# Tokenizer tower on one core: the weight stage's residual conv as column-half pairs, image stores in pieces

## The reference, cut to what matters

```python
x = patches(x)                      # 784 patches of 3x16x16, normalised by their own mean and deviation
x = conv3x3(x, conv1_w) ; residual = x
x = gelu(group_norm(x)) ; x = conv3x3(x, rconv1_w)
x = gelu(group_norm(x)) ; x = conv3x3(x, rconv2_w)
x = residual + x
x = conv(x, proj_w, stride=16)      # 192 numbers a patch
... embeddings, one causal attention block, one two-branch transformer block
```

## Time and profile before

| what | us |
|---|---|
| median of 3 runs | 1586.49 (1581.76 to 1587.44) |
| profiled execution | 1585.12 |
| its span, first to last instruction | 1583.3 |
| first matmul of the weight stage | 14.24 |
| last matmul of the weight stage ends | 246.2 |
| first conv1 of the main stage | 248.96 |
| PE busy over the span | 1429.4 (90%) |

### The profile page before, as it was taken

One profiled execution on the slowest core, in us unless ns is written; L12 is line 12 of the kernel. 1 busy time (PEld: TensorE's weight loads), 2 busy tenths in 40 slices (PEclk: granted clock), 3 DMA queues, 4 the chain that ended last, 5 costly groups with the idle time before them and its releaser, 6 DMA issues. The chain is left out here.

```text
span 1583.3 us, 42709 instructions
## 1 busy us (share of the span) xinstructions
PE 1429.4 (90%) x13490; PEld 1008.6 (64%) x13490; DVE 1134.6 (72%) x4227; ACT 837.4 (53%) x2102; POOL 581.8 (37%) x1111
## 2 busy tenths in 40 slices
PE   6969996888999999989999998999999766978889
PEld 2424442333688588858877875888588666655647
DVE  7723334999988888888888887888888750474710
ACT  1212222777777676766767666666767501333442
POOL 2000003555544455444454544445554401161500
PEclk9989997999999999999999999999999887987999
DMA  6463325433555455445545553554555577300000
GB/s 181 122 205 88 99 87 220 100 101 101 138 148 143 123 150 143 131 121 145 144 119 151 146 140 101 149 147 128 139 144 143 160 202 167 71 1 1 2 3 14
DMA packets 117219, 190.63 MB, mean 120 GB/s; under 512 B 18252, under 2 KB 86284, under 8 KB 116942
## 3 DMA queue, kind: packets, MB, share of 16 engines
q1 hardware_dynamic: 117070, 188.60, 43.6%
HBM read 103.34 MB, written 21.30 MB: 79 GB/s over the span
## 5 line engine op out<-in xcount | busy, mean ns | idle before, releaser
L363 POOL TENSOR_TENSOR sb_tmp<-sb_mst,sb_half_neg 128x8 f32<-128x8 f32 x200 | 354.6, 1773 | 684.4 <-DVE sb_mst L789 684.4
L501 PE MATMUL rc<-sb_acts,sb_rwd 128*64 128x512 f16 x1764 | 563.5, 392 | 18.3 <-DMA sb_acts<-sb_hst 18.2
L502 PE MATMUL rc<-sb_acts,sb_rwd 128*64 128x512 f16 x1764 | 564.7, 393 | 0.0
L417 ACT ACTIVATE sb_f32q<-c,sb_gsh,sb_gsc 128x128 f32<-128x128 f32 x792 | 298.2, 458 | 285.6 <-POOL sb_gsh L373 285.6
L501 PE MATMUL rc<-sb_acts,sb_rwl 128*64 128x512 f16 x1176 | 363.9, 391 | 5.2 <-issue 5.2
L502 PE MATMUL rc<-sb_acts,sb_rwl 128*64 128x512 f16 x1176 | 363.4, 391 | 0.0
L556 PE MATMUL pj<-sb_wall,sb_arena 128*64 128x384 f16 x1792 | 309.9, 337 | 21.7 <-DMA sb_wall<-w_lo 15.1
L425 ACT ACTIVATE sb_g2f<-rc,sb_gsh,sb_gsc 128x128 f32<-128x128 f32 x784 | 297.3, 481 | 4.4 <-POOL sb_gsh L373 4.4
L560 PEld LDWEIGHTS pj<-sb_wall,sb_arena 128*64 128x64 f16 x1792 | 219.0, 222 | 63.8
L560 PE MATMUL pj<-sb_wall,sb_arena 128*64 128x192 f16 x1792 | 240.9, 247 | 0.0
L556 PEld LDWEIGHTS pj<-sb_wall,sb_arena 128*64 128x64 f16 x1792 | 215.5, 219 | 38.8 <-DMA sb_wall<-w_lo 16.4
(11 more groups left out here) (158 smaller groups left out, 1726.2 us busy)
## 6 DMA issues: line engine op xcount, KB each, us to landing
sb_acts<-sb_hst SPq DMA_DIRECT2D x792, 78.8 KB, 2.6
sb_wall<-w_lo SPq DMA_DIRECT2D x56, 528.0 KB, 3.8
sb_im<-x_planes SPq DMA_DIRECT2D x202, 136.5 KB
sb_wall<-w_lo SPq DMA_DIRECT2D x28, 480.0 KB, 3.7
sb_f32q<-in_proj SPq DMA_DIRECT2D x12, 576.0 KB, 3.9
sb_arena<-in_proj SPq DMA_DIRECT2D x12, 576.0 KB, 4.4
w_lo<-sb_arena SPq DMA_DIRECT2D x1, 6144.0 KB, 17.3
scratch_fold<-sb_wall SPq DMA_DIRECT2D x48, 123.8 KB
```

The source lines that it names most:

```text
L363: ch.did(gp.tensor_tensor(t1, var, half_neg[:, :], ALU.pow))
L417: ins = nc.scalar.activation(g1f[:, q * Q + m, :], c1[q][:, m * HALF:(m + 1) * HALF], ACT.Gelu, bias=gsh[q][:, m:m + 1], scale=gsc[q][:, m ...
L501: nc.tensor.matmul(out[0:CH, :], w_odd, x_odd, start=(n == 0), stop=(n == 14))
L502: yield nc.tensor.matmul(out[CH:128, :], w_even, x_even, start=(n == 0), stop=(n == 14))
```

## The change

- **Residual conv** (`fold_pairs`): for each half, 15 pairs of matmuls in place of 18. Each pair is one matmul into partitions 0 to 63 of the bank and one into 64 to 127, each with 64 columns of weights. The first 6 pairs read only the low rows (slot 2 of `acts[p]`). The other 9 read the high rows, which stand in `acts[p]` doubled: slot 0 holds the image rows of one parity in both partition halves, slot 1 those of the other.
- **High rows**: ACT makes them now (`proj_hi`), into one buffer `hfull` for all units. SP copies them by four transfers of 64 partitions x 1296 (`double_proj`). DVE keeps the low part alone. `proj_hi` waits for the unit's load, and that the unit before has been split and doubled; in ACT's loop it stands between the two evacuations of `rc` and those of the projection. PE waits for the doubling (`s_fdup`) after the sixth pair of half 0.
- **SP** is written out for all units: double n + 1, load n + 2, store n.
- **Image stores** in 21 pieces: three for `scratch_x` after the stores of units 5, 6, 7, and eighteen of one plane each, one or two after each of units 9 to 20. The zero tiles come after unit 22. DVE splits the planes in three portions.
- **Weights**: two more transfers of parameters; `fdup` and `tdup` are doubled forms. POOL clears `hfull` and slot 2 at the stage's end.

```diff
-            def fold_io(i, p, last):
-                n = 2 * i + p
-                if not last:
-                    sp.wait_ge(s_psp, 2 * n + 2)
-                    load_proj(n + 2, p)
+            def double_proj(n):
+                p = n % 2
+                sp.wait_ge(s_psh, n + 1)
+                if n >= 2:
+                    sp.wait_ge(s_tps, n - 1)
+                for row, half in ((0, 0), (1, 1), (0, 1), (1, 0)):
+                    sp.dma_start(acts[p][64 * half:64 * half + 64, row, 0:U * PAD],
+                                 hfull[64 * row:64 * row + 64, :]).then_inc(s_fdup, 16)
+
+            def store_t(n):
+                p = n % 2
                 sp.wait_ge(s_tev, 3 * n + 3)
...
+            double_proj(0)
+            for n in range(FU - 1):
+                double_proj(n + 1)
+                if n + 2 < FU:
+                    sp.wait_ge(s_psp, n + 1)
+                    load_proj(n + 2, n % 2)
+                store_t(n)
+                if 5 <= n < 8:
+                    store_piece(n - 5)
+                if 9 <= n < 21:
+                    for m in range(18 * (n - 9) // 12, 18 * (n - 8) // 12):
+                        store_piece(C + m)
...
+            def proj_hi(i, p, wait=True):
+                n = 2 * i + p
+                act.wait_ge(s_pld[p], 16 * (i + 1))
+                if wait:
+                    act.wait_ge(s_psp, n)
+                    act.wait_ge(s_fdup, 64 * n)
+                nc.scalar.activation(hfull[:, :].rearrange("p (r x) -> p r x", x=WD * Q)[:, :, Q:(P + 1) * Q],
+                                     stage[p].rearrange("p (r x) -> p r x", x=P * Q), ACT.Copy, scale=WS).then_inc(s_psh, 1)
...
+                if more:
+                    proj_hi(i + 1, p)
                 if not first:
                     act.wait_ge(s_ts[p], 32 * i)
                 act.wait_ge(s_tps, n + 1)
...
+                    conv = fold_pairs(rc[p][q], acts[p], q)
+                    run(conv, 6)
+                    if q == 0:
+                        pe.wait_ge(s_fdup, 64 * (n + 1))
+                    run(conv).then_inc(s_fold, 1)
...
-                v.tensor_scalar(hi, src, WS, None, ALU.mult).then_inc(s_psp, 1)
-                dve.wait_ge(s_psp, 2 * n + 1)
                 v.scalar_tensor_tensor(lo, src, WS, hi, ALU.mult, ALU.subtract).then_inc(s_psp, 1)
```

More of the change, by code:

```diff
@@ L95, in build_front @@
         acts = [sb(f"acts_{i}", [128, 3, HB], F16) for i in range(2)]
[L96 to L97 removed]
+        hfull = sb("hst", [128, U * PAD], F16)
+        hst = [hfull[:, q * Q * PAD:(q + 1) * Q * PAD] for q in range(2)]
         g2f = sb("g2f", [128, U, HALF])
@@ L258, in load_im @@
                                          ap=[[1, 3], [PLANE, 18], [1, RUN]])).then_inc(s_im[p], 16)
[L260 to L263, removed]
+            sp.wait_ge(s_scr, 16 * STORES)
             load_im(0, 0)
             load_im(1, 1)
-            for p in range(2):
-                fold_io(FU // 2 - 1, p, True)
+            store_t(FU - 1)
             sp.wait_ge(s_wlo, 2 * FU)
@@ L468, in _ @@
         def _(pe):
[L469 to L480, removed]
             def run(gen, count=None):
@@ L502, in pairs, with fold_pairs, rows, wl @@
                     yield nc.tensor.matmul(out[CH:128, :], w_even, x_even, start=(n == 0), stop=(n == 14))
+            def fold_pairs(out, buf, q):
+                def rows(k, t, m):
+                    v = buf[:, k, q * Q * PAD:(q + 1) * Q * PAD].rearrange("p (r x) -> p r x", r=SL)
+                    return v[:, t:t + 8, m * Q:(m + P) * Q]
+                def wl(kind, m):
+                    return fwl[:, (3 * kind + m) * CH:(3 * kind + m + 1) * CH]
+                def wd(ky, m):
+                    return fwd[:, (3 * ky + m) * CH:(3 * ky + m + 1) * CH]
+                low = ((wl(0, m), rows(2, 1, m), wl(2, m), rows(2, 0, m)) for m in range(3))
+                edge = ((wl(1, m), rows(2, 0, m), wl(3, m), rows(2, 1, m)) for m in range(3))
+                odd, even = ((1, 0), (0, 1), (1, 1)), ((0, 0), (1, 0), (0, 1))
+                high = ((wd(ky, m), rows(*odd[ky], m), wd(ky, m), rows(*even[ky], m)) for ky in range(3) for m in range(3))
+                for n, (w_odd, x_odd, w_even, x_even) in enumerate(itertools.chain(low, edge, high)):
+                    nc.tensor.matmul(out[0:CH, :], w_odd, x_odd, start=(n == 0), stop=(n == 14))
+                    yield nc.tensor.matmul(out[CH:128, :], w_even, x_even, start=(n == 0), stop=(n == 14))
             def fold_step(i, p, first):
                 n = 2 * i + p
-                pe.wait_ge(s_psp, 2 * n + 2)
+                pe.wait_ge(s_psp, n + 1)
                 for q in range(2):
@@ L726, in _, with image_split @@
             dve.wait_ge(s_xz, 1)
-            for q in range(6):
+            def image_split(q):
                 c, pr = q // 2, q % 2
@@ L735, in _ @@
                 v.tensor_tensor(dst[1], src, dst[0], ALU.subtract).then_inc(s_xhl, 1)
-            with dve.Fori(2, FU // 2 - 1) as i:
+            for i in range(2, 5):
+                image_split(2 * i - 4)
+                image_split(2 * i - 3)
+                fold_pair(i)
+            with dve.Fori(5, FU // 2 - 1) as i:
                 fold_pair(i)
@@ L1524, in layout @@
     o["tband"] = tb.reshape(128, TP)
+    o["tdup"] = np.stack([np.concatenate([tb[h], tb[h]]) for h in range(2)], 1).reshape(128, 2 * TP)
     wb = np.zeros((KC, 2, CH), w1.dtype)
```

117 lines of the change are left out of this document (66 added, 51 removed).

## The result

| what | before | after |
|---|---|---|
| median of 4 runs each, us | 1584.85 (1581.76 to 1587.44) | 1626.13 (1622.69 to 1630.80) |
| ratio, 95% interval | | 1.0263 (1.0225 to 1.0302) |
| profiled execution | 1585.12 | 1629.21 |
| its span | 1583.3 | 1627.4 |
| weight stage ends | 246.2 | 281.4 |

The change costs 2.6%. I forecast 1620; it is 1626, inside the range, and 9.2 us above the forecast if profiled executions are compared. The span is 44.1 us longer: 35.2 of it stand in the weight stage, 3.2 in the gap before conv1, 5.7 behind it.

The account below looks back on a forecast made before the run. A chain from load to load through ACT and SP, 10.1 us, bounds the weight stage; 21 of these, the start, the last unit and 18 us of pieces end it 34.9 us later: 1585.12 becomes 1620 us, range 1597 to 1650.

Parts of the forecast that it names:

- The bound moves into a ring: Weight stage: a chain from one load's issue through ACT and SP to the next load's, 10.1 us (9.4 to 11.0).
- The backlog: Weight stage: each load stands behind four doublings in the queue, 0.4 us (bounds 0 and 1.3).
- The pieces: Weight stage: 21 image-store pieces on SP between a store and the doublings, 18 us (10 to 25).
- The start: Start of the weight stage: first preparing operation at 9.0 instead of 7.71, load of unit 2 issued at 32.2.
- The end: Weight stage's end to the main stage's first conv: nothing longer; about 8 us on SP fits beside unit 23.
- the cold start: Weight stage: after the tensor engine's idle at the seventh pair, a lower clock costs 2.0 us, taken by slack; nothing.
- slack as told: Weight stage: the tensor engine's work on a unit ends 5.9 us before ACT's next work could wait for it.
- Rival 3: Weight stage: the clock falls at the new wait and stays down, unit 11.4 us, 1647 us; chance 0.12.
- Rivals 1 and 2: Weight stage: tensor engine stays the bound, 1561 us, chance 0.05; or cheap doubling issue and no backlog, 1579 us, chance 0.08.

Follow-up runs that it names:

- the engine-bound version: Kernel after with the projection evacuated first, two of four doublings made as DVE copies, and zero tiles after units 8 and 21: 1550.44 us, ratio 0.9778.

## Why the prediction was right

**The bound moves into a ring: right.** Loads come 9.87 us apart, against 10.1. The terms, from the unit shown: landing with its wake-up and backlog 4.33 (forecast 4.1 + 0.4 + 0.1), high rows and evacuations 1.82 (1.94; the high rows alone 1.16, forecast 1.17), to SP 0.03 (0.21), stores 0.82 (0.79), doublings and step 2.44 (2.61). The landing varies most, and this ring has the shortest of the five: their mean until ACT may begin is 4.70, forecast 4.6. That each link is one is shown by the runs that take it out (evacuation, two doublings), not by the sum. One reading of the old kernel was off without harm: the load issued at 221.84 is that of unit 23, which the engine needs one unit after 228.43, so 15 us later and not 7.

**The backlog: a term that hit by luck.** I put 0.4 us on the load for standing behind four doublings, and the mean landing is about that much longer than in the earlier trace rows. But without two of them it landed no sooner, and in front of them 2 us later. What makes it longer is open.

**The pieces: mis-sized.** 18 us forecast, 24.3 measured (22.0 with the plain ring of 9.98), near the upper bound of 25. The three of `scratch_x` lengthened their rings by 8.1 (37.7 for three rings against 3 x 9.87), the ring after them by 0.7, the eighteen planes theirs by 15.5, or 0.86 each, where the price by bytes was 0.91. I had put my value between issue and bytes; bytes was the answer, and most of it is paid on SP: behind a `scratch_x` piece the doublings take 1.8 us longer to issue. With two planes in a ring, SP needs 1.3 us more from store to load (146.86 to 150.62, against 2.44), and the ring is about 1.9 longer.

**The start: 1.5 us too late.** 8.38 instead of 9.0, small transfers from 12.99, the first load in the ring at 30.68, not 32.2. The order of events was as told.

These errors cancel, which is luck: the start -1.5 us, the plain rings -4.8, the pieces +6.3. Twenty-one rings and the pieces took 231.6, forecast 230.1, and the load of unit 23 went out at 262.27, forecast 262.3; the stage ended at 281.4, forecast 281.1.

**The end: this step failed.** Up to the first conv "nothing gets longer by my reckoning", I wrote; it was 3.2 us longer. The chain from the store of unit 22 to conv1 is 0.76 for the store, 2.80 for the zero tiles, 1.28 until they have landed, 3.12 for issuing the image loads and 4.42 until conv1 starts, together 12.4. I had 0.79, 3.0, 2.6 and 2.6, which is 9.0, and nothing for the landing of the image windows. The chain also began later. By my own numbers unit 22 is through 8.7 us after the load of unit 23, at 271.0, and its store goes out behind the doublings, near 272.5, which would just have fitted. It went out at 274.99, 6.4 us before the stage's end: unit 22, at a granted clock of 0.50 in its first 5 us, took 8.6 us from its first high pair where I had 6.3. Twelve pairs at 0.42 instead of 0.22 are 2.4 us of that, an estimate from the rows of the profile that no run separates. So the cold start, which I put at nothing, costs nothing within the rings, but here, behind the last load, nothing covers it. In the three kernels with four of the zero tiles after unit 8 conv1's idle time is 2.8 again, released by DVE; in the kernels of the new order without that it is 4.6 to 6.3.

**Behind conv1: 5.7 us that I didn't forecast, most of it not told from spread.** From conv1 to the end the profiles of the new order take between 1332.6 and 1342.8 us (the kernel after 1340.0), the two of the old order 1334.3. What all of the new order share is a slower beginning: the first pair that needs high rows comes 20.16 us after conv1 instead of 18.43 (19.4 to 21.2 in the others). The 6 MB of low weights are in the queue there, landing in 22.6 us instead of 17.3, and the granted clock over the first 24 us is 0.50 instead of 0.64. Which of the two it is, no run shows.

**The tensor engine: slack as told.** It is idle 26 of 120 us. The granted clock fell in many units (0.89 over the stretch) and up to the last units nothing came later for it: ACT's evacuation of the projection waits for the engine only twice, 0.2 us each, in units 22 and 23. Rival 3 needed a unit of over 10.1 and did not come. Rivals 1 and 2 fell with the ring itself: issuing a doubling costs 0.60, not 0.38. Rival 1's sum, 1561, lies near what the engine-bound version reached (1550), which shows the distance that was at stake.

## What to carry to other kernels

When an edit adds a step between a transfer's landing and the next transfer's issue, follow the order lists around in a circle and add up the links; if the circle is longer than the busiest engine's unit, it sets the time, however idle each engine is. Then look for what stands in the circle only by its place in a list: moving one evacuation ahead of a wait was worth 59 us here, and took the stores and pieces with it. What follows the last round of the circle needs a sum of its own, down to the last landing: there the slack that covers a late engine inside the circle is gone. Half of a doubling that stays in its own partitions is a copy, not a transfer.

## What the runs showed of the hardware

**First in the queue is not first to land.** A load of 576 KB with four doublings of 162 KB ahead of it on the same queue landed in 4.3 to 4.4 us (evacuation first), and in 6.5 to 7.7 with the doublings right behind it; the doublings themselves went from 2.9 to 4.5. Counted from the first of the five issues to the last landing the two orders are near each other: 2.4 + 4.9 = 7.3 in the kernel after, and 7.5 to 8 in the one with the load first. It looks as if all five ended together when the load goes first. The Trainium skill, "DMA: Bandwidth & Descriptors", section "Queues, rings and completion order", says that descriptors are consumed in ring order but that completion is not first in, first out for an issuing engine. The second half agrees with these landings: the first doubling is issued 0.6 us behind the load and lands after 4.5, the load after 6.5 to 7.7. The first half alone would not let me expect that a later transfer delays an earlier one by 2 to 3 us. Why it does is open.

**Issuing is held up by what is in flight.** Four doublings take 2.39 us to issue, 4.19 behind a piece of 784 KB, eight of them 15.61 while the image load runs and 8.36 otherwise (with a wait for the second unit's high rows in both). Rival 1 of the prediction cites the Trainium skill, "DMA: Bandwidth & Descriptors", section "Issuing engines are not separate DMA queues", that issuing is usually small beside the transfer. For one doubling that is so here (0.60 us, against 3.4 to landing). But four stand one behind the other in the ring, and with two issues fewer per unit the stage was 29 us shorter.
